# A fused attention and FFN kernel: shared quads with score, maximum and value products side by side

## What is computed

```
x: (8, 256, 512), mask: (8, 512), Wq, Wk, Wv: (256, 256)
Q, K, V = W @ x, 16 heads of 16 channels, 512 positions
att = softmax(mask(Q K^T / 4 + b));  y = att V            # (8, 256, 512)
Wg, Wu: 4096 x 512, Wd: 512 x 4096, dequantised from 4-bit codes, a scale for each 32
out = x + (gelu_tanh(y Wg^T) * (y Wu^T)) Wd^T             # over the last axis, 2048 rows
```

## Time and profile before

| | us |
|---|---|
| median of 3 runs | 1584.52 (1582.51 to 1585.08) |
| the profiled execution | 1589.26 |
| its span, first to last instruction | 1587.5 |
| from the start to the first FFN product | 219.2 |
| chunk 0 | to 600.4 |
| chunk 1 | to 967.9 |
| chunk 2 | to 1318.9 |
| chunk 3 | to the end |

### The profile page before, as it was taken

One profiled execution on the slowest core, in us unless ns is written; L12 is line 12 of the kernel. 1 busy time (PEld: TensorE's weight loads), 2 busy tenths in 40 slices (PEclk: granted clock), 3 DMA queues, 4 the chain that ended last, 5 costly groups with the idle time before them and its releaser, 6 DMA issues.

```text
span 1587.5 us, 18889 instructions
## 1 busy us (share of the span) xinstructions
PE 1474.7 (93%) x7376; PEld 548.1 (35%) x7376; DVE 690.8 (44%) x934; ACT 739.4 (47%) x843; POOL 310.9 (20%) x242
## 2 busy tenths in 40 slices
PE   3778779999999999999999999999999999999998
PEld 1122223333333332333333333333343333444443
DVE  5667667766677543444333333333333311111111
ACT  2246556756575654565455454644454551111110
POOL 3001124333345311111011111111111111111110
PEclk8598899999999999999999999999999999999999
DMA  5130325333343331432232230432222222323220
GB/s 177 48 96 18 87 86 183 120 119 117 133 164 130 120 123 56 137 101 81 75 115 111 68 108 12 147 107 101 80 81 80 80 81 91 121 80 145 95 80 27
DMA packets 51129, 157.91 MB, mean 99 GB/s; under 512 B 7632, under 2 KB 21072, under 8 KB 50912
## 3 DMA queue, kind: packets, MB, share of 16 engines
q1 hardware_dynamic: 48192, 153.80, 28.4%
q10 hardware_dynamic: 2848, 2.90, 0.5%
HBM read 118.64 MB, written 37.77 MB: 99 GB/s over the span
## 4 chain that ended last, share of the span: by engine, by line
PE 79%; ACT 4%; DMA 4%; DVE 4%; issue 3%; POOL 2%; SPq 2%; ACTq 1%; POOLq 0%; DVEq 0%
PE psum L890 14%; PE psum L891 12%; PE psum L892 12%; PE psum L938 8%; PE psum L939 7%; PE psum L940 7%; PE psum L860 6%; PE psum L830 5%; PE psum L846 4%; DMA wide<-seed_rows 2%; PE psum L806 2%; ACT big L627 2%; POOL dq_w L394 1%; ACTq L387 1%; DVE w_ring L408 1%
## 5 line engine op out<-in xcount | busy, mean ns | idle before, releaser
L890 PE MATMUL psum<-y_hi,w_ring 128*128 128x512 f16 x1024 | 395.2, 386 | 19.3 <-POOL y_lo L509 15.8
L627 ACT ACTIVATE big<-psum 128x1024 f32<-128x1024 f32 x256 | 260.0, 1023 | 326.2 <-PE psum L846 314.8
L891 PE MATMUL psum<-y_lo,w_ring 128*128 128x512 f16 x1024 | 391.9, 383 | 0.0
L892 PE MATMUL psum<-y_hi,w_ring 128*128 128x512 f16 x1024 | 391.8, 383 | 0.0
L694 DVE TENSOR_REDUCE maxima<-psum 128x2 f32<-128x1024 f32 x179 | 219.0, 1223 | 253.9 <-PE psum L830 253.7
L521 POOL TENSOR_TENSOR in_lo<-inter,in_hi 128x512 f16<-128x512 f32 x128 | 149.4, 1167 | 851.6 <-ACT in_hi L609 851.6
L742 DVE SCALAR_TENSOR_TENSOR inter<-psum,gelu 128x512 f32<-128x512 f32 x128 | 88.3, 690 | 325.2 <-PE psum L892 309.1
L938 PE MATMUL psum<-w_ring,in_hi 128*128 128x512 f16 x512 | 197.4, 386 | 5.2 <-POOL in_lo L521 2.7
L939 PE MATMUL psum<-w_ring,in_hi 128*128 128x512 f16 x512 | 195.8, 382 | 0.0
L940 PE MATMUL psum<-w_ring,in_lo 128*128 128x512 f16 x512 | 195.5, 382 | 0.0
L752 DVE SCALAR_TENSOR_TENSOR acc<-psum,acc 128x512 f32<-128x512 f32 x128 | 88.4, 691 | 207.8 <-PE psum L940 206.1
(11 more groups left out here) (69 smaller groups left out, 971.6 us busy)
## 6 DMA issues: line engine op xcount, KB each, us to landing
w_ring<-w_parts SPq DMA_DIRECT2D x96, 768.0 KB, 7.2
w_parts<-w_ring SPq DMA_DIRECT2D x32, 768.0 KB, 3.3
dq_scales<-scales SPq DMA_DIRECT2D x32, 384.0 KB
wide<-qk_parts SPq DMA_DIRECT2D x64, 128.0 KB
qk_parts<-wide SPq DMA_DIRECT2D x60, 128.0 KB
dq_packed<-packed SPq DMA_DIRECT2D x32, 192.0 KB
small<-x SPq DMA_DIRECT2D x8, 512.0 KB, 4.3
wide<-qk_parts SPq DMA_DIRECT2D x64, 64.0 KB
```

Source lines behind the costliest of these rows:

```text
L627: nc.scalar.activation(p_exp[:, k, :, i], p_score[:, bank:bank + 2, :], ACT.Exp, scale=SCORE_SCALE).then_inc(exp_done, 1)
L890: nc.tensor.matmul(dst, w[:, 0, k % 2, cols], hi, start=(k == 0), stop=False)
L891: nc.tensor.matmul(dst, w[:, 0, k % 2, cols], lo, start=False, stop=False)
L892: return nc.tensor.matmul(dst, w[:, 1, k % 2, cols], hi, start=False, stop=(k == TT - 1))
```

## The change

Batches 0 and 1 keep `PLAN`. From batch 2 on, another table, `SHARED_PLAN`, orders the steps, in which a bar marks where FFN steps go; `on_pe` is gone. Each quad has 16 bars, and each bar gets three FFN steps (two in the first fifth of chunk 0), 48 in a quad. Score products, a pair of maximum products and, in half of the cases, value products stand in a row with no bar between, then come two bars. The transposes `MT` and `Y` stand together. `F0` stands in quad 1 and `G1` in quad 2, each a quad earlier than before.

```diff
+        SHARED_PLAN = (
...
+            "X S00 m m A2 | K0a | S01 m m A3 | K0b | K0h AO S10 m m K0l | | S11 m m | MT Y MH ML YN | S20 m m A0 | MV F0 | "
+            "S21 m m | Q1a | S30 m m A1 | Q1b | Q1h S31 m m Q1l | |",
...
+        )
-        def plan(g, first, last):
+        def plan(g, first, last, shared):
...
-            for step in PLAN[g].split():
+            for step in (SHARED_PLAN if shared else PLAN)[g].split():
...
-                    for step, arg in plan(g, b == 0, b == B - 1):
+                    for step, arg in plan(g, b == 0, b == B - 1, b >= SOLO):
...
-            for step in ("A2", "A3", "AO", "Y", "YN"):
+            for step in "| A2 | A3 | AO | | Y | YN".split():
...
-        def on_pe(step):
-
-            return step[0] in "SmAY" and step not in ("AO", "YN") or step == "MT" or step[0:2] in WORK and step[2] in "ab"
...
-                left = sum(on_pe(step) for _, _, step, _ in span)
+                left = sum(step == "|" for _, _, step, _ in span)
...
-                    if on_pe(step):
+                    if step == "|":
```

## The result

The changed kernel takes 1525.75 us (median of 4 runs, 1522.85 to 1528.77), the kernel before 1584.8 us beside it; the ratio is 0.9629, with a 95% interval of 0.9607 to 0.9652. It is 59 us faster. The forecast was 1538.5 us in a range of 1521 to 1558.

The account below looks back on a forecast made before the run. The prediction took PE's own row of instructions as the bound while FFN and attention share it. Terms -44 - 4 + 1 + 1 = -46 us from the 1584.5 us median gave 1538.5 us, range 1521 to 1558.

Parts of the forecast that it names:

- 0.30 x 88 + 0.20 x 87 + 0.6 = 44 us: PE's row during the FFN: gains from score, maximum and value products standing together, 26.4, 17.4 and 0.6 us.
- The distance of 0.23 us: Start of score pair to start of maximum pair on PE; up to 0.32 us would take 16 us from the gain.
- the rivals of chunk 0: Chunk 0 clears up, 1521.5 us, chance 0.12; or chunk 0 jams, 20 us more, about 1558 us, chance 0.12.
- neighbours: Attention products in a row on PE save about 0.1 us per way in and out: 44 us less.
- waits of chunk 0, y left out: PE's waits in chunk 0 stay about 20 us, with 1 us put on top; bounds -17 and +20.
- waits for exponentials, chunks 1 and 2: Two FFN blocks between score pairs take away 4 of 5.1 us of PE's waits; bounds 0 and 5.
- ends of chunks 0 and 1: PE's wait for the split of y gets 0.5 us longer, twice: 1 us; bounds -2 and +3.
- the rival that chunk 0 clears up: Room for ACT and DVE makes chunk 0's 19.9 us of waits nearly vanish: 1521.5 us, chance 0.12.
- The fills: Ten DMAs each on SP's queue; filling earlier removes no wait and costs nothing.
- A0 waiting for the normalising: Value products wait for DVE to normalise y; at 3 us in each of 23 quads 1607.5 us, chance 0.03.

Follow-up runs that it names:

- the run with all apart: Changed kernel with one FFN step put between score and maximum pairs and one between maximum pair and value products: 1568.55 us, 0.9893 of the kernel before.
- the changed kernel's second trace: The unchanged changed kernel run again as the mark beside three other kernels: 1524.97 us, ratio 0.963.
- 17 for two bars: Kernel with y's split ahead of x's (1517.71 us), each FFN chunk starting two bars later and two bars behind YN at attention's end: 1535.02 us, 0.9675.
- The drop to 1502.89 us: Changed kernel with x's split last, value products in pairs behind S00 and S20, and chunks starting one bar later: 1502.89 us, ratio 0.9468.

## Why the prediction was right, and where it was off

The direction, the mechanism and the largest term were right. The step "0.30 x 88 + 0.20 x 87 + 0.6 = 44 us" is 43.6 us by the run with all apart, and its two parts, forecast at 9 to 10 and 35 us in the expectations, are 10.6 and 35.6. The distance of 0.23 us between scores and maxima, taken from one place ahead of the FFN, stands in the changed kernel's chunk 1 too.

The Trainium skill (TensorE: Matmul & The Clock Gate, Part 3) states that weight loads to the same row groups don't overlap with running products. That does not show here: with it the distance would have been longer than 0.23 us.

The Trainium skill (TensorEngine Tiling (Array Packing), Key Properties) also states that a change of the tiling mode drains TensorE. The trace fits that: the losses of 0.1 us lie at the ways between products of 53 or 51 rows, of 128 rows, and of 32 columns, and none lies between 53 and 51 rows. That a drain is what costs them no run shows. One way is open in it: a transpose of maxima, whose weights have 16 columns, starts 0.22 us behind an FFN product (22 places), without a loss.

What was off is the rest, -2 us in the forecast and about -16 us in the measurement. The measured 1525.75 us lies 2 us outside the forecast's own range of 1528 to 1550; it is inside 1521 to 1558 because that range was drawn to hold the rivals of chunk 0. One of the signs failed with it: chunk 0 was to wait 15 to 25 us, y left out, and waits 13.3. By the terms, in the profiled executions (1589.3 and 1526.6 us):

| term | forecast | measured |
|---|---|---|
| neighbours | -44 | -43.6 (run with all apart) |
| waits of chunk 0, y left out | +1 | 13.3 - 19.9 = -6.6 |
| waits for exponentials, chunks 1 and 2 | -4 | -5.1 |
| ends of chunks 0 and 1 | +1 | +0.4 |
| low clock | not in the sum | seven stretches to two, 4 x 1.7 + 2.8 = up to 9.6 less |
| before the FFN | 0 | 221.8 - 219.2 = +2.6 |
| sum | -46 | -62 of the 62.7 |

The 43.6 us come from another pair of runs, and are a net: the run with all apart waits 3.7 us less than the changed kernel beside it. As a check, what is left of the 62.7 us without waits (11.3), clock (9.6) and start (+2.6) is 44.4 us. The start is no effect of the change that two runs agree on: the changed kernel's second trace has its first FFN product at 220.0 us.

- The mis-sized term is chunk 0. I took the waits of the second half of the chunk, found that the new order is as dense everywhere, and kept 20 us. But half of those waits were for exponentials, and all of them are gone, in chunk 0 as in the others. This is the rival that chunk 0 clears up: at a third of its size by the waits, and at two thirds with the three stretches at the low clock that were behind them (5 us). The forecast also took 48 FFN steps for each quad of the chunk; the first has 32.
- The missing term is the clock, the largest miss of the sum. The rows showed it (the record of 0.61 us at 600.38 where others have 0.38), and I did not price what a wait of 3 us costs behind itself.
- The fills were priced at nothing, which was right against the kernel before and wrong as a statement on the new order: they keep 17 us away.
- The rival on the slower side, A0 waiting for the normalising, exists: six waits, 6.5 us in all, in chunk 0, and none in chunk 1 or 2. It was priced at 69 us if it came at 3 us in each quad. The reason given against it, that DVE is busy 133 of 367 us in chunk 1, fits that split; in chunk 0 it is busy 259 of 355.
- The ends of the chunks went as forecast in sign, at 4.2 us for the 4.5 given.

What stays open: why chunk 0 reacts so strongly to the place of the FFN steps and value products (15 us for value products moved to S21, 17 for two bars). Who waits for whom is named, but ACT's row was not followed step by step through a quad, and a version in which ACT never comes late was not found. The drop to 1502.89 us has no cause that is shown.

## What to carry to other kernels

On an engine that is never idle, read the starts, not the durations: the price of going from one kind of product to another stands between the starts, and multiplied by the number of visits it forecast 44 us to within 1. When a reordering is judged, price a wait of some 2 us or more with what may follow it, 1.7 us of lower clock and more here. And where transfers are issued from a queue that also waits for other things, bringing the reader forward can ask for bringing the transfer forward too: here 17 us of the gain hung on it.

## What the runs showed of the hardware that I had not expected

- Whether the low clock follows a wait is no matter of that wait's length alone. Behind waits for y of 4.2 us it sets in (0.61 over the first 3.7 us of chunk 1). Behind the wait of 2.74 us at the start of chunk 3 the kernel before has 0.58 over 4.1 us, and the changed kernel, with the same wait of 2.74 us, 1.00 over 4.2 us. One and the same program does both: behind the wait of 2.72 us for the last down products, the changed kernel's first trace has 0.53 over 3.6 us and its second 1.00. The start of chunk 3 and that place in the first trace, then that place in the second:

```profile
1257.80:1262.00 4.20, 4.13 (x20) 1.89 (x21) 0.00 (x0) 0.60 (x1) 1.12 (x2) 1.00 0.00 0
1509.40:1513.00 3.60, 3.60 (x9) 1.29 (x10) 0.00 (x0) 0.00 (x0) 0.00 (x0) 0.53 0.00 0
```

```profile
1508.40:1512.00 3.60, 3.57 (x17) 1.67 (x18) 0.69 (x1) 0.00 (x0) 0.00 (x0) 1.00 0.00 0
```

The Trainium skill (TensorE: Matmul & The Clock Gate, Part 1) says that an idle TensorE falls back to half its clock. The long waits agree, the short ones do so in some places and runs and not in others.

- Two groups of value products in a row take 1.86 us, two apart 2 x 1.00: a way out costs 0.14 us there.
